# A decoder layer on one core: the first normalisation of batches 1 to 3 on VectorE, the drain of self-attention in another order, first scores over four banks

## The reference, cut to what matters

```python
x = layernorm(x + attn(x, W_K, W_Q, W_V, W_O))      # 16 heads of 128, causal
x = layernorm(x + gamma * cross(x, ctx, ctx))       # 8 heads of 64, softmax over 512
x = layernorm(x + ffn(x, W_g, W_u, W_d))            # ternary weights, 2048 hidden
```

## Time and profile before

| | us |
|---|---|
| median of 3 runs | 1494.51 (1493.49 to 1495.16) |
| the profiled execution, its own time | 1496.47 |
| its span, first to last instruction | 1494.7 |
| granted TensorE clock, mean | 0.983 of full |
| self-attention | 0 to 991 of the span |
| cross-attention | 991 to 1230 |
| FFN | 1230 to the end |

### The profile page before, as it was taken

How to read it: one execution, slowest core, us unless ns; L and a number is a source line. 1 busy time by engine, 2 the same in 40 slices (tenths; PEclk the granted TensorE clock), 3 DMA queues, 4 the chain that set the end, 5 groups by cost and what they waited for, 6 DMA issues and landing times. The chain is left out here.

```text
span 1494.7 us, 23730 instructions
## 1 busy us (share of the span) xinstructions
PE 1438.2 (96%) x7008; PEld 1149.2 (77%) x7008; DVE 1071.8 (72%) x2324; ACT 716.8 (48%) x1535; POOL 653.1 (44%) x507
## 2 busy tenths in 40 slices
PE   7999999999999999999999999878998989999996
PEld 6788888888888888888888888757787865565564
DVE  4667677776777676767776767677787895796854
ACT  3444444535444444444444444356787863333332
POOL 1343525334344344352444352566767543343432
PEclk9999999999999999999999999989999998999999
DMA  7466666666666666566566665744456613000000
GB/s 193 134 182 183 179 177 176 193 162 179 172 182 177 175 175 186 158 190 182 169 174 180 184 177 156 217 135 106 128 136 163 175 43 113 1 29 28 0 29 28
DMA packets 205034, 213.97 MB, mean 143 GB/s; under 512 B 98752, under 2 KB 172480, under 8 KB 204992
## 3 DMA queue, kind: packets, MB, share of 16 engines
q1 hardware_dynamic: 203840, 212.93, 51.1%
q10 hardware_dynamic: 1152, 0.52, 0.2%
HBM read 125.83 MB, written 79.69 MB: 138 GB/s over the span
## 5 line engine op out<-in xcount | busy, mean ns | idle before, releaser
L667 ACT ACTIVATE probs<-probs,neg_max 128x128 f32<-128x128 f32 (+3 forms) x256 | 142.4, 557 | 357.8 <-DVE neg_max L796 350.3
L475 POOL TENSOR_TENSOR v_lo<-placed,v_hi 128x512 fp32r<-128x512 f32 x63 | 81.9, 1299 | 350.7 <-ACT v_hi L673 350.7
L477 POOL TENSOR_TENSOR pT_lo<-placed,pT_hi 128x1280 fp32r<-128x1280 f32 x63 | 186.5, 2960 | 0.0
L856 DVE SCALAR_TENSOR_TENSOR acc<-bank,prob_recip,acc 128x512 f32<-128x512 f32 x256 | 174.8, 745 | 6.0 <-PE bank L560 1.1
L1521 POOL TENSOR_TENSOR prod_lo<-prod,prod_hi 128x512 fp32r<-128x512 f32 x64 | 84.5, 1320 | 143.3 <-ACT prod_hi L1630 143.3
L796 DVE CUSTOM_DVE_ANT_0 probs<-bank,mask 128x128 f32<-128x128 f32 (+3 forms) x256 | 117.1, 481 | 8.2
L771 DVE TENSOR_TENSOR qT_lo<-bank,qT_hi 128x512 fp32r<-128x512 f32 x64 | 44.2, 691 | 104.8 <-ACT qT_hi L655 104.8
L1073 POOL TENSOR_SCALAR xprobs<-xprobs,xprob_recip 128x512 f32<-128x512 f32 x128 | 87.4, 703 | 69.5 <-DVE xprob_recip L1294 69.5
L808 DVE STREAM_TRANSPOSE turned<-probs 128x256 f32<-128x256 f32 (+1 forms) x384 | 114.0, 363 | 0.0
L1580 PE MATMUL bank<-wdT_f32r,prod_hi 128*128 128x512 f32 x256 | 109.9, 429 | 2.1 <-POOL prod_lo L1521 1.6
L1223 ACT ACTIVATE xprobs<-bank,xneg_max 128x512 f32<-128x512 f32 x128 | 88.9, 695 | 43.8 <-DVE xneg_max L1283 42.9
(11 more groups left out here) (159 smaller groups left out, 3862.9 us busy)
## 6 DMA issues: line engine op xcount, KB each, us to landing
turned_scratch<-turned SPq DMA_DIRECT2D x64, 896.0 KB, 3.8
placed<-turned_scratch SPq DMA_DIRECT2D x252, 224.0 KB, 4.2
cp<-context_halves SPq DMA_DIRECT2D x64, 256.0 KB, 3.9
...
```

Source lines behind the costliest of these rows:

```text
L477: nc.gpsimd.tensor_tensor(pT[par][1][:], landed_probs(landing), pT[par][0][:].bitcast(F32), ALU.subtract).then_inc(p_lo, 1)
L667: nc.scalar.activation(probs[:, cols], probs[:, cols], ACT.Exp, bias=low[:, par, t:t + 1], scale=-1.0, accum_out=total[:, par, t:t + 1]).t ...
L856: nc.vector.scalar_tensor_tensor(out=acc[:, b * NT + t, :], in0=s_bank[t][:], scalar=recip[:, b, t:t + 1], in1=acc[:, b * NT + t, :], op0= ...
```

## The change

Four edits.

1. `apply_norm` is now a VectorE instruction. For batch 0 the three tiles come in the drain, behind `values_lo`. For batches 1 to 3 there is one tile in each of the first four heads of the batch ahead, at the second unit of the head. The statistics of batch b + 2 move to units 17, 21, 25 and 29 of batch b, the variance to 30; rstd is computed on GpSimd at the end of head 7.
2. SP loads the context's first four tiles in the items of head 14, and the load of `W_u` of head 15 stands between item 62's write to DRAM and its read.
3. ScalarE makes z's high part of item 62 ahead of the halves of item 63.
4. Score units 0 to 9 go round four banks (units 4 to 9 wait for the exponential of unit v - 4), and unit 2 moves ahead of the output of item 63, with its maximum on VectorE.

```diff
--- before.py
+++ after.py
@@ -393,6 +393,10 @@
 
         def loads(h, b, more):
 
+            if not more:
+                for name in {1: ("wk", "wq"), 2: ("wv",), 3: ("wo",)}.get(b, ()) if h < H - 1 else ():
+                    sp.wait_ge(w_turn[name], H)
+                    rows.load_tile(sp, 0, tuple(raw).index(name))
             if b == 0:
                 wait_apart(sp, k, f_turn, h * 3 + 1)
                 load_gate_up(sp, "wg", h)
@@ -429,12 +433,8 @@
                 step(h, b, True)
         for b in range(B):
             step(H - 2, b, False)
-        for t, name in enumerate(("wk", "wq", "wv", "wo")):
-            sp.wait_ge(w_turn[name], H)
-            rows.load_tile(sp, 0, t)
         loads(H - 1, 0, False)
-        exchange(FIRST + 2, 0, landing=1)
-        loads(H - 1, 1, False)
+        exchange(FIRST + 2, 0, lambda: loads(H - 1, 1, False), landing=1)
         loads(H - 1, 2, False)
         exchange(FIRST + 3, 1)
         keep_signs(H - 1, 0)
@@ -505,9 +505,6 @@
         halves_lo(FIRST + 2, 0, 1)
         norm_gpsimd(nc, pool, norm, k.minus_half, 0)
         halves_lo(FIRST + 3, 1)
-        pool.wait_ge(norm.rstd_ready, 1)
-        for t in range(1, NT):
-            cross.apply_norm(pool, 0, t)
         rows.split(nc, pool, halves, k, H - 1)
         pool.wait_ge(rows.split_done, H + 1)
         cross.begin_gpsimd(pool)
@@ -634,18 +631,18 @@
         pe.wait_ge(logits_ready, ITEMS * NT)
         output_product(FIRST, 0)
         output_product(FIRST + 1, 1)
+        pe.wait_ge(v_turn, ITEMS)
         values_product(FIRST + 2, 2, Z_BANK[2])
-        pe.wait_ge(v_turn, ITEMS)
         for pair in range(2):
             cross.transpose_values(pe, pair)
         output_product(FIRST + 2, 0)
         for pair in range(2, 4):
             cross.transpose_values(pe, pair)
         values_product(FIRST + 3, 3, Z_BANK[3])
-        for unit in range(2):
+        for unit in range(3):
             cross.scores(pe, unit)
         output_product(FIRST + 3, 1)
-        for unit in range(2, 8):
+        for unit in range(3, 8):
             cross.scores(pe, unit)
         pe.wait_ge(o_added, H * B * NT)
         cross.begin_tensor(pe)
@@ -755,8 +752,8 @@
         z_hi_of(1)
         sign(H - 1, 1)
         sign(H - 1, 2)
+        z_hi_of(2)
         halves_hi(FIRST + 3, 1)
-        z_hi_of(2)
         for pair in range(2):
             cross.values_hi(act, pair)
         cross.first_queries_hi(act)
@@ -902,9 +899,11 @@
         cross.first_queries_lo(dve)
         for pair in range(2, 4):
             cross.values_lo(dve, pair)
+        for t in range(1, NT):
+            cross.apply_norm(dve, 0, t)
         add_outputs(FIRST + 2, 2)
         z_lo_of(3)
-        for unit in range(2):
+        for unit in range(3):
             cross.row_max(dve, unit)
         add_outputs(FIRST + 3, 3)
         cross.begin_vector(dve)
@@ -941,7 +940,7 @@
 
 
     S_AHEAD, PT_AHEAD = 10, NT - 2
-    NORM1_STATS, NORM1_VAR, NORM1_APPLY = (2, 9, 16, 23), 26, {6: (0, 1), 7: (2, 3)}
+    NORM1_STATS, NORM1_VAR = (17, 21, 25, 29), 30
     nat, nat_loaded = source.nat, source.nat_loaded
     ITEMS, UNITS = B * XH, B * XH * NT
     PAIRS = XH // 2
@@ -969,6 +968,12 @@
     recip_ready, probs_ready = sem("xrecip_ready"), sem("xprobs_ready")
     pt_full, pt_hi, pt_lo = sem("xpt_full"), sem("xpt_hi"), sem("xpt_lo")
     z_full, z_scaled, z_added = sem("xz_full"), sem("xz_scaled"), sem("xz_added")
+
+    BEGIN_BANKS = (bank[1], bank[2], bank[3], bank[0])
+
+    def bank_of(v):
+
+        return BEGIN_BANKS[v % 4] if v < S_AHEAD else score_bank[v % 2]
 
     def ahead(b, h, d):
 
@@ -1056,10 +1061,10 @@
             last = nc.gpsimd.memset(val[p][:, :, :, 1:3, :].bitcast(F32), 0.0)
         last.then_inc(zeroed, 1)
 
-    def apply_norm(pool, b, t):
+    def apply_norm(dve, b, t):
 
         tile = tile_of(b, t)
-        nc.gpsimd.tensor_scalar(tile, tile, norm1.mv[:, t, 0:1], norm1.rstd[:, t:t + 1], ALU.subtract, ALU.mult).then_inc(applied, 1)
+        nc.vector.tensor_scalar(tile, tile, norm1.mv[:, t, 0:1], norm1.rstd[:, t:t + 1], ALU.subtract, ALU.mult).then_inc(applied, 1)
 
     def queries_lo(pool, b, pair):
 
@@ -1079,8 +1084,6 @@
         normalise(pool, 1, 1)
         norm_gpsimd(nc, pool, norm1, k.minus_half, 1)
         pool.wait_ge(norm1.rstd_ready, 2)
-        for t in range(NT):
-            apply_norm(pool, 1, t)
 
     def gpsimd(pool):
         def step(b, h):
@@ -1094,12 +1097,9 @@
                 wait_apart(pool, k, z_scaled, b * PAIRS + (h // 2 + 3))
                 tile = tile_of(b, h // 2)
                 nc.gpsimd.tensor_tensor(tile, z_gamma[:], tile, ALU.add).then_inc(z_added, 1)
-            if normalises(b) and h == min(NORM1_APPLY):
+            if normalises(b) and h == XH - 1:
                 norm_gpsimd(nc, pool, norm1, k.minus_half, b + 2)
-                wait_apart(pool, k, norm1.rstd_ready, b + 3)
-            if normalises(b):
-                for t in NORM1_APPLY.get(h, ()):
-                    apply_norm(pool, b + 2, t)
+                pool.wait_ge(norm1.rstd_ready, b + 3)
             if is_item(b, h, B - 1, 0):
                 norm_gpsimd(nc, pool, quant.norm2, k.minus_half, 0)
             if is_item(b, h, B - 1, 3):
@@ -1123,8 +1123,10 @@
 
     def scores_tile(pe, b, h, t, v):
 
-        if v > 1:
+        if v >= S_AHEAD:
             pe.wait_ge(exp_done, v - 1)
+        elif v >= 4:
+            pe.wait_ge(exp_done, v - 3)
         if t == 0:
             pe.wait_ge(source.halves_loaded[h % 2], b * (32 * PAIRS) + 32 * (h // 2 + 1))
             if v < 2 * NT:
@@ -1132,7 +1134,7 @@
             else:
                 pe.wait_ge(xs_loaded[h % 2], b * (32 * PAIRS) + 32 * (h // 2))
         for p in range(2):
-            last = nc.tensor.matmul(score_bank[t % 2][:], xs[h % 2][:, t * P:(t + 1) * P], cp[h % 2][:, p, :],
+            last = nc.tensor.matmul(bank_of(v)[:], xs[h % 2][:, t * P:(t + 1) * P], cp[h % 2][:, p, :],
                                     start=(p == 0), stop=(p == 1))
         last.then_inc(scores_full, 1)
 
@@ -1220,7 +1222,7 @@
     def exp_tile(act, v, q, t):
 
         act.wait_ge(max_ready, v + 1)
-        nc.scalar.activation(probs[q][:, t, :], score_bank[t % 2][:], ACT.Exp, bias=negmax[:, q, t:t + 1],
+        nc.scalar.activation(probs[q][:, t, :], bank_of(v)[:], ACT.Exp, bias=negmax[:, q, t:t + 1],
                              accum_out=total[:, q, t:t + 1]).then_inc(exp_done, 1)
 
     def turned_hi(act, u, jt):
@@ -1280,7 +1282,7 @@
 
     def tile_max(dve, v, q, t):
         dve.wait_ge(scores_full, v + 1)
-        nc.vector.tensor_reduce(negmax[:, q, t:t + 1], score_bank[t % 2][:], AX.X, ALU.max, negate=True).then_inc(max_ready, 1)
+        nc.vector.tensor_reduce(negmax[:, q, t:t + 1], bank_of(v)[:], AX.X, ALU.max, negate=True).then_inc(max_ready, 1)
 
     def row_max(dve, v):
         tile_max(dve, v, v // NT, v % NT)
@@ -1302,7 +1304,7 @@
 
     def begin_vector(dve):
         start_at_one(nc, k, z_scaled, z_scaled, z_added)
-        for v in range(2, S_AHEAD):
+        for v in range(3, S_AHEAD):
             row_max(dve, v)
             u = v - (S_AHEAD - PT_AHEAD)
             if u >= 0:
@@ -1362,6 +1364,9 @@
                     turned_lo(dve, u + PT_AHEAD, (j + PT_AHEAD) % NT)
                 if j == 2 and exists(m + 2, ITEMS):
                     reciprocals(dve, m + 2, (h + 2) % 4)
+                if j == 1 and h < NT and exists(b + 1, B):
+                    dve.wait_ge(norm1.rstd_ready, b + 2)
+                    apply_norm(dve, b + 1, h)
                 beside(b, h * NT + j)
             if values_follow(b, h):
                 pair_lo(dve, b, h // 2)
```

## The result

The changed kernel takes 1472.62 us (median of 4 runs, 1468.23 to 1474.04), the kernel before 1494.84 beside it: ratio 0.985, 95% interval 0.982 to 0.987. A second set with the same code, on another chip, gave 0.987 (0.985 to 0.989). The forecast was 1471, within 1465 to 1482. The profiled execution took 1472.45 us, span 1470.5, granted clock 0.992.

A forecast was written before the change was run, and what follows sets the result against it. TensorE, busy 96% of the span, was taken as the bound, with time winnable only where it idles or clocks low. Drain 4.6, head 1.2 and batches 17.6 sum to 23.4 us, giving 1471 us, range 1465 to 1482.

The forecast's parts named there:

- the three places: Items 2 to 4, 10 to 12 and 18 to 20, said to lose 19.1 us behind GpSimd's normalisation tiles.
- Applies in the batches: Batches 1 to 3: hidden at 0.53 us each, except three meeting GpSimd at unit 1; 1.5 us given back, bounds 0 and 6.
- Net in the batches: Cross-attention batches: 19.1 us of removed stalls less 1.5 given back, 17.6 us won.
- SP's queue: Drain: loads moved from ahead of item 62's write end VectorE's DMA waits; additions of item 60 start 4.7 us earlier.
- ScalarE's order: Drain: z's high part of item 62 made first removes VectorE's 1.46 us pause before z_lo of item 62.
- Three applies in the drain: On VectorE ahead of z_lo of item 63, covered by nothing: cost 1.6 us, up to 5.0.
- Four banks: Head: first scores no longer wait for an exponential; 1.2 us won, bounds 0 and 3.
- A: Rival: the drain gives nothing, its gains taken back by transfers, applies or later waits; 1476 us, chance 0.18.
- B: Rival: many of the 15 applies wait for GpSimd at the port lock and TensorE is delayed; 1482 us, chance 0.14.
- C: Rival: slower than before, each apply waiting out two GpSimd instructions, 3.09 us seen by TensorE; 1514 us, chance 0.03.
- D: Rival: nothing changes, the batches' losses having another cause and another wait taking their place; 1494 us, chance 0.03.
- E: More won: TensorE's clock stays high in the drain and the batches give nothing back; 1467 us, chance 0.12.

The follow-up runs named there:

- the batches' part alone: Kernel before with only the twelve applies of batches 1 to 3 on VectorE and their statistics moved: ratio 0.989, 14.1 us below the kernel before.
- four columns: Changed kernel with the batches' twelve applies cut to the first four of 512 columns: ratio 0.986 to the kernel before, items 2 to 24 in 149.06 us.
- that part alone: Changed kernel with batches 1 to 3's applies back on GpSimd and statistics at the old units: ratio 0.997, 4.7 us below the kernel before.
- the two halves by themselves: Two kernels, one with only the batches' edits, one with only the drain and first-score edits: 14.1 and 4.7 us below the kernel before.

## Why the prediction was right, and where not

- **What bounds the kernel; the cause in the batches.** Right. GpSimd's tiles of 2.08 us were what VectorE and TensorE stood behind; with them moved, the three places are gone, and the batches' part alone gives 14.1 of the whole 19 to 23.
- **"These three places lose 9.10, 5.37 and 4.67 us, 19.1 us in all."** Too large, the one main term that was mis-sized. The undisturbed stretch was read on the engine that the stalls had displaced; by exponentials it is 17.4 in that profile, and 16.1 and 16.8 in two others with the same batches.
- **Applies in the batches, 1.5 given back.** Near in size; the mechanism is not shown. The three stretches now take 13.94, 13.85 and 13.84 us by exponentials, 1.2 over 3 x 13.47. But they are still 0.7 over with the applies at the fourth unit, where none lost more than 0.03, and 0.7 over with four columns, and 0.8 in the changed kernel's second profile. So at most half of the 1.2 is the meeting with GpSimd that was priced; the rest is open. In the first profile a further 1.0 was lost in the two long stretches (41.07 and 40.81 for 40.40 and 40.45); 17.4 - 1.2 - 1.0 makes 15.2, and the table has 15.35.
- **Net in the batches, 17.6.** Items 2 to 24 won 16.1 on the mean of the seven profiles with this part unaltered (148.99) against three with it as before (165.12), 15.35 in the first pair. The bet that applies in GpSimd's pauses cost 0.54 held nine times in twelve. Beside GpSimd's `normalise` they cost hardly more, 0.57 at most, as its instructions are short and the applies came late in them; there GpSimd loses 0.16 to 0.27 each time instead.
- **SP's queue, 4.7.** The mechanism is right, the size is 3.3 on the mean (2.0 to 4.4): the waits were 4.8 to 6.3 us, by execution, and more than 1.3 came back, part of it in the wait for ScalarE that was late next.
- **ScalarE's order, 1.46.** Measured 0.34; in part counted twice, with the step before.
- **Three applies in the drain, 1.6.** 1.45 measured, 1.4 on the path. Not foreseen: tile 0's apply, 1.02 us before, met GpSimd's `pT_lo` earlier and took 1.63.
- **Four banks, 1.2.** 1.2 to 2.7 at a like clock, nothing in the first profile.
- **The drain and head together, 5.8.** 5.56 in the first pair, 4.7 by the runs of that part alone. From sign_u to item 2 it takes 66.97, 64.19 and 66.71 us with the old drain and 60.17 to 61.68 in seven profiles of the new one, 5.0 less on the mean. The drain's misses have different signs, and partly cancel.
- **The rivals.** A fell (0.997, interval below 1). B was met at three of twelve applies and tile 0's, far from its 10.9 us. C and D fell. E had the clock in the drain staying high and nothing given back in the batches; in the head the clock was 0.92 before and 0.78 after, and 0.91 in the second profile, and no ratio came down to its 0.982.

The total of 1472.6 for 1471 is thus right in its main term. The first pair of profiles flattered it, 3.3 us of clock in the tail hiding most of what was missing. The medians stand 22.2 us apart in the first set and 19 to 21 in the second, where 23.5 were forecast, and the two halves by themselves add to 18.8. The second set's 0.987 is the more cautious figure.
